# Expert tiles in turns over all experts, with the first batch's pooling begun between the last tiles

## The reference

```python
x = x + mamba4(lap(x))                 # 4 layers: conv, selective scan over the 256 positions, 16 states
r = concat(gelu(x@W1+b1)@W2+b2, h@We[id]+be[id])       # a per-batch conditioned MLP
w, e = top_k(r @ gate, 2); w = softmax(w)              # each token picks 2 of 8 experts
x = x + sum_k w_k * (silu(r@w0[e_k]) * (r@w1[e_k])) @ wo[e_k]
s = tanh(x@cW1+cb1) @ cv                               # pooling logits, one per position
p = softmax(where(mask(kind[b]), s, -1e30)); pooled = p@x / count
x = x + attention(pooled)              # 16 heads of 64, causal, low rank K and V, then @ w_out
c = x@cw[id].T + cb[id]; x = x + bitlinear(gelu(bitlinear(c, w1)), w2)   # ternary weights, 8-bit activations
```

## Time and profile before

| | |
|---|---|
| median of three runs | 1354.98 us (1354.03 to 1356.9) |
| span of the profiled execution, first to last instruction | 1353.1 us |
| busy PE, DVE, ACT, POOL | 1279.3 (95%), 1116.8 (83%), 1019.1 (75%), 1101.0 (81%) us |
| mean granted PE clock | 0.997 |
| scans and routing | 0 to 883 us |
| expert tiles | 883 to 996 us |
| from the last tile to the first projection | 996 to 1017 us |
| attention and last MLP | 1017 to 1353 us |

### The profile page before, as it was taken

One profiled execution on the slowest core, in us unless ns is written; L12 is line 12 of the kernel. 1 busy time (PEld: TensorE's weight loads), 2 busy tenths in 40 slices (PEclk: granted clock), 3 DMA queues, 4 the chain that ended last, 5 costly groups with the idle time before them and its releaser, 6 DMA issues.

```text
span 1353.1 us, 20591 instructions
## 1 busy us (share of the span) xinstructions
PE 1279.3 (95%) x5755; PEld 735.0 (54%) x5764; DVE 1116.8 (83%) x1636; ACT 1019.1 (75%) x2552; POOL 1101.0 (81%) x647
## 2 busy tenths in 40 slices
PE   8899999999999999999999999999998999999997
PEld 4344344344344344344344355789985666676666
DVE  4999999999999999999999989655545566665655
ACT  4888888988988988888888887533326787887785
POOL 5799999999999999999999997454427766857562
PEclk9999999999999999999999999999999999999999
DMA  6564164254254344344435362523221000000000
GB/s 206 224 250 189 64 269 189 88 234 188 103 230 188 138 183 188 153 180 202 173 133 227 164 188 68 156 53 95 69 60 29 9 21 16 22 17 17 9 5 13
DMA packets 48870, 169.49 MB, mean 125 GB/s; under 512 B 15448, under 2 KB 33052, under 8 KB 40460
## 3 DMA queue, kind: packets, MB, share of 16 engines
q1 hardware_dynamic: 46508, 163.81, 31.4%
q0 software_dynamic: 2272, 4.66, 1.6%
HBM read 160.78 MB, written 7.67 MB: 124 GB/s over the span
## 4 chain that ended last, share of the span: by engine, by line
PE 39%; DVE 26%; issue 17%; ACT 12%; POOL 4%; DVEq 1%; DMA 1%; POOLq 0%; ACTq 0%; SPq 0%
DVE h L1479 18%; DVE h L1460 5%; PE banks L424 5%; ACT banks L1441 5%; PE banks L771 4%; PE banks L844 4%; PE banks L818 4%; POOL h L1485 3%; PE banks L433 3%; PE banks L711 2%; PE banks L1514 2%; PE banks L748 2%; PE banks L728 2%; PE banks L859 2%; ACT L1312 2%
## 5 line engine op out<-in xcount | busy, mean ns | idle before, releaser
L1485 POOL TENSOR_TENSOR h<-h,Cb 128x1024 f32<-128x1024 f32 (+2 forms) x166 | 581.5, 3542 | 8.8 <-DVE h L1479 8.3
L1479 DVE TENSOR_TENSOR_SCAN h<-banks,h 128x1024 f32<-128x1024 f32 x256 | 568.7, 2270 | 5.6 <-ACT banks L1441 4.3
L1441 ACT ACTIVATE banks<-dt,A_cur 128x255 f32<-128x255 f32 x1024 | 424.1, 462 | 73.8 <-DVE h L1479 70.9
L1514 PE MATMUL banks<-h,ident 128*128 128x512 f32 x1024 | 471.4, 600 | 4.1 <-DVE yz L1523 1.4
L1514 PEld LDWEIGHTS banks<-h,ident 128*128 128x128 f32 x1024 | 186.7, 190 | 240.0 <-issue 197.6
L1460 DVE TENSOR_TENSOR h<-Bb,banks 128x1024 f32<-128x1024 f32 (+2 forms) x101 | 199.7, 1995 | 0.6
L1466 POOL TENSOR_TENSOR h<-Bb,u 128x1024 f32<-128x1024 f32 (+1 forms) x50 | 184.1, 3685 | 1.9 <-DVE xs L1382 1.8
L810 POOL TENSOR_SCALAR h<-h 128x128 f32<-128x128 f32 (+1 forms) x128 | 97.7, 779 | 53.1 <-DVE h L794 53.1
L810 POOL TENSOR_SCALAR Cb<-Cb,h 128x128 f32<-128x128 f32 x124 | 94.7, 780 | 36.4 <-DVE h L794 36.2
L1268 PE MATMUL banks<-xn,wF 128*128 128x512 f32 x256 | 113.0, 592 | 2.2 <-ACT xn L1260 2.2
L1268 PEld LDWEIGHTS banks<-xn,wF 128*128 128x128 f32 x256 | 47.4, 188 | 63.5 <-issue 60.3
(11 more groups left out here) (393 smaller groups left out, 2048.4 us busy)
## 6 DMA issues: line engine op xcount, KB each, us to landing
Cb<-scrX SPq DMA_DIRECT2D x32, 2048.0 KB, 9.0
Bb<-scrX SPq DMA_DIRECT2D x31, 2048.0 KB, 13.0
h<-in_L_ffn_w SPq DMA_DIRECT2D x2, 2048.0 KB, 8.7
by_expert<-Cb SPq DMA_DIRECT2D x39, 64.0 KB, 1.5
h<-in_conv_w SPq DMA_DIRECT2D x4, 512.0 KB, 4.2
Bb<-scrX SPq DMA_DIRECT2D x2, 1024.0 KB, 5.7
scr<-Cb SPq DMA_DIRECT2D x3, 640.0 KB, 3.0
wF<-scr SPq DMA_DIRECT2D x3, 512.0 KB
```

Of the source, the lines that this page charges most:

```text
L1441: m = e.activation(ps_dA[c % 2][:, g, half, 1:S], dts[q][:, half, i * S + 1:(i + 1) * S], ACT.Exp, scale=A_cur[q][:, s:s + 1])
L1479: e.tensor_tensor_scan(chunk(i, c), ps_dA_flat[c % 2], chunk(i, c), 0.0, ALU.mult, ALU.add).then_inc(sem("scan"), 1)
L1485: e.tensor_tensor(h[i][:, rows(cs), :, :], h[i][:, rows(cs), :, :], both(Cb[i], cs), ALU.mult).then_inc(sem("hC"), len(cs))
L1514: m = e.matmul(bank(5), ident[:], h_flat[i][:, s * HALVES * S:(s + 1) * HALVES * S], start=(s == 0), stop=(s == NS - 1))
```

## The change

Tiles are walked in turns: first the first tile of every expert, then every expert's second, and so on. For that the counting makes, for each pair (expert, n-th list), a number saying whether that list is used and its place in the walk; a comparison with the tile's number and three matmuls give each tile its list and its expert's weights. POOL has three steps instead of six, ACT one copy more, PE one matmul more and five fewer.

A tile's result is stored at the place of its list (read from `tl_col` by SP), not in order of tiles. So a token's place is known from its rank alone, and `dve_homes` is one copy. Tiles without rows go to seven spare places. Before that, 15 DMAs, one in each slot from the second, fill `by_expert` with rows of x (9 places of 64 KB, 590 KB each) on SP's queue behind the second `spread_B`; the first store waits for them.

Since a batch has 256 tokens, its rows are in the first two lists of each expert, so batch 0's lie in the first 16 tiles and batch 1's in the first 32. POOL picks batch 0's rows behind the gathers of tiles 21 and 23, once 16 tiles are stored, and batch 1's behind those of tiles 36 and 38, once 32 are. DVE sums batch 0 behind tile 25 and does its `pmax` before tile 30; PE makes `x2t`, `at` and `S` of batch 0 ahead of `up` of tiles 28, 29 and 30, ACT its parts there. PE waits for what reads banks 4 and 5 before it turns the next tile into them. The hardware loop covers tiles 6 to 17, and tiles 18 to 35 are written out. Two masks and the first conditioned weights are loaded after tile 21.

Behind the last tile PE runs `fold`, `pturn`, `pool`, `q:0`; `heat` and `hold` are gone. `levels`, without its first step, stands on DVE between `pool` and `k:0`. On ACT the exp table and `pexp` stand ahead of `fold`. The slots begin at −2.

```diff
+            def mask(b):
+                kind = e.value_load(ids[0:1, B + b:B + b + 1], min_val=0, max_val=2)
+                wait(e, sem("pch"), 2 * b - 3)
+                dma(chosen[b % 2], layer_of(io["pmask"], kind), f"pk{b % 2}")
+
+            def conditioned(b):
+                sid = e.value_load(ids[0:1, b:b + 1], min_val=0, max_val=NE - 1)
+                wait(e, sem("f_c"), b)
+                dma(fcw, layer_of(io["cw"], sid), "cw")
+                dma(fcb, bass.AP(io["L1_cond2_bias"].tensor, sid * P, [[0, P], [1, P]]), "cw")
+
+            e.wait_ge(sem("table"), 3)
+            e.wait_ge(sem("ys0"), FILLED)
...
             for t in range(TILES):
+                col = e.value_load(tl_col[0:1, t:t + 1], min_val=0, max_val=PLACES - 1)
                 e.wait_ge(sem("mo_o"), t + 1)
-                dma(by_expert[t * P:(t + 1) * P, :], mo_out[t % TRIPLE], f"ys{t % TRIPLE}")
+                dma(layer_of(by_place, col), mo_out[t % TRIPLE], f"ys{t % TRIPLE}")
                 if t == 2 * TRIPLE:
                     dma(f1raw, io["f1t"], "fw_in")
                     dma(f2raw, io["f2t"], "fw_in")
@@ -355,28 +387,19 @@
                 elif t == 6 * TRIPLE:
                     dma(Wq, io["L1_attn_w_q"], "aw_in")
                     dma(Wo, io["L1_attn_w_out"].rearrange("(c p) o -> p c o", p=P), "aw_in")
+                elif t == 7 * TRIPLE:
+                    mask(0)
+                    mask(1)
+                    conditioned(0)
...
+            mask(2)
...
+            e.memset(lists_[:, P:PLACES], 0.0).then_inc(sem("const"), 1)
+            e.wait_ge(sem("const"), CONSTS + 1)
             e.wait_ge(sem("table"), 1)
             for t in range(TILES):
                 k = t % TRIPLE
-                col = e.value_load(tl_col[0:1, t:t + 1], min_val=0, max_val=P - 1)
+                col = e.value_load(tl_col[0:1, t:t + 1], min_val=0, max_val=PLACES - 1)
                 if t == 0:
                     e.wait_ge(sem("by_tok"), 16 * NPAIR)
                     e.wait_ge(sem("table"), 2)
                 wait(e, sem("mo_xt"), t - 2)
                 e.tensor_copy(list_now[:, k:k + 1], lists[:, bass.ds(col, 1)]).then_inc(sem("const"), 1)
-                e.wait_ge(sem("const"), CONSTS + t + 1)
+                e.wait_ge(sem("const"), CONSTS + t + 2)
                 e.indirect_dma_start(xg[k], None, by_token, bass.IndirectOffsetOnAxis(ap=list_now[:, k:k + 1], axis=0)
                                      ).then_inc(sem(f"xg{k}"), 16)
+                if t in GATHER_AFTER:
+                    b, part = divmod(GATHER_AFTER.index(t), 2)
+                    if part == 0:
+                        stored(e, (b + 1) * HALF_TILES)
+                        e.wait_ge(sem("pos"), 1)
+                    gp_gather(e, b, part)
+            stored(e, TILES)
+            run(e, "gp", ATT_GP)
+
+
+        def stored(e, tiles):
             for k in range(TRIPLE):
-                e.wait_ge(sem(f"ys{k}"), 16 * (TILES // TRIPLE))
-            e.wait_ge(sem("pos"), 1)
-            run(e, "gp", ATT_GP)
-
+                e.wait_ge(sem(f"ys{k}"), (0 if k else FILLED) + 16 * len(range(k, tiles, TRIPLE)))
...
+                if isinstance(t, int) and t in FRONT_PE:
+                    PIECES["pe"][FRONT_PE[t]][1](e, 0)
...
+                    if isinstance(t, int) and t in FRONT_READ:
+                        e.wait_ge(sem(FRONT_READ[t][0]), FRONT_READ[t][1])
...
-            with e.Fori(1, TILES // TRIPLE // 2) as j:
+            with e.Fori(1, FRONT // 2) as j:
                 tiles(j * 2, 0)
                 tiles(j * 2 + 1, 1)
+            for j in range(FRONT, TILES // TRIPLE - 1):
+                tiles(j, j % 2)
...
+                    if isinstance(t, int) and t in FRONT_ACT:
+                        PIECES["act"][FRONT_ACT[t]][1](e, 0)
...
+                    if isinstance(t, int) and t == FRONT_MAX:
+                        PIECES["dve"]["pmax"][1](e, 0)
                     tile_mul(t, k, (k + odd) % 2)
                     if not (last and k):
                         tile_weights(t + 2, (k + odd) % 2)
                     if not (isinstance(t, int) and t == 0):
                         tile_out(j - (0 if k else 1), t - 1, (k - 1) % TRIPLE, (k - 1 + odd) % 2)
+                    if isinstance(t, int) and t == FRONT_COMB:
+                        PIECES["dve"]["comb"][1](e, 0)
...
-            weights_levels(e, r)
             e.sem_inc(sem("f_o"), 2)
-            chained.append(r.base + r.k)
-            chained.pop(0)
+            e.wait_ge(sem("fws_ps"), 1)
+            r(e.tensor_scalar(fsm[:, 10:12], bank(5, 2), 1.0 / FF, Q_EPS, ALU.mult, ALU.max))
+            chain[0] = r
+            chained[0] = r.base + r.k + LEVEL_STEPS
             run(e, "dve", ATT_DVE)
 
-        def weights_levels(e, w):
-            e.wait_ge(sem("fws_ps"), 1)
-            w(e.tensor_scalar(fsm[:, 10:12], bank(5, 2), 1.0 / FF, Q_EPS, ALU.mult, ALU.max)); w.sync()
+        def dve_levels(e, b):
+            w = chain[0]
+            w.sync()
...
-            if b == 1:
-                e.wait_ge(sem("x2T"), 2)
-            elif b == 2:
+            if b == 2:
...
+        def front(b, step):
+            return bank(4 if b else 4 + (FRONT_X2T + step) % 2)
...
+            def fill(t):
+                e.dma_start(by_expert[(t - 1) * FILL_PLACES * P:t * FILL_PLACES * P, :], x_rows[0:FILL_PLACES * P, :]
+                            ).then_inc(sem("ys0"), 16)
...
+                    fill(t)
...
             counts = [run_tot[1]] + [tot16[:, t * NE:(t + 1) * NE] for t in range(*GROUPS[2])]
-            row, column = bank(TABLE_BANK)[:, 0:NE], bank(TABLE_BANK)[0:NE, NE:NE + 1]
             for k, here in enumerate(counts):
-                e.matmul(column, here, ones_w[:, 0:1], start=(k == 0), stop=(k == len(counts) - 1))
-            for k, here in enumerate(counts):
-                m = e.matmul(row, ones_w, here, start=(k == 0), stop=(k == len(counts) - 1))
+                m = e.matmul(bank(TABLE_BANK)[0:NE, 2:3], here, ones_w[:, 0:1], start=(k == 0), stop=(k == len(counts) - 1))
...
+        def pe_spread(e, _):
+            e.wait_ge(sem("sums"), 1)
+            e.matmul(bank(TABLE_BANK)[:, 0:1], spread_w, count16, start=True, stop=True).then_inc(sem("rank"), 1)
+
         def pe_ahead(e, _):
-            e.wait_ge(sem("sums"), 1)
-            e.wait_ge(sem("need"), 3)
-            e.matmul(bank(TABLE_BANK)[0:NE, NE + 1:NE + 2], upper_w[0:NE, 0:NE], need16, start=True, stop=True
-                     ).then_inc(sem("rank"), 1)
+            e.wait_ge(sem("sums"), 2)
+            e.wait_ge(sem("need"), 1)
+            e.matmul(bank(TABLE_BANK)[:, 1:2], upper_w, used16, start=True, stop=True).then_inc(sem("rank"), 1)
...
+            n(e.tensor_scalar(used16, counted[:, 0:1], rcon[:, RC_FULL:RC_FULL + 1], None, ALU.is_gt))
+            n(e.tensor_scalar(unused, counted[:, 0:1], rcon[:, RC_FULL:RC_FULL + 1], FAR, ALU.is_le, ALU.mult))
+            e.wait_ge(sem("sums"), 3)
+            n(e.tensor_tensor(turn_no, counted[:, 1:2], unused, ALU.add))
...
+            e.tensor_scalar(hot16, tile_no, turn_no, None, ALU.is_equal).then_inc(sem("need"), 1)
 
         def pe_tiling(e, _):
             e.wait_ge(sem("need"), SPAN_STEPS + 1)
-            e.wait_ge(sem("sums"), 2)
-            got = bank(TABLE_BANK)[:, 2 * NE:2 * NE + 2 * TILES]
-            e.matmul(got[:, 0:TILES], room_w, tq16, start=True, stop=True)
-            e.matmul(got[:, TILES:2 * TILES], ones_w[0:NE, :], tq16, start=True, stop=True).then_inc(sem("rank"), 1)
+            for k, weights in enumerate((ones_w[:, 0:1], place_w, offset_w)):
+                m = e.matmul(tile_table(k), weights, hot16, start=True, stop=True)
...
+        def dve_homes(e):
             e.tensor_copy(pos, place).then_inc(sem("pos"), 1)
...
+            r(e.scalar_tensor_tensor(out=t2[0:1, :], in0=tile_table(0), scalar=-1.0,
+                                     in1=rcon[0:1, RC_SPARE:RC_SPARE + TILES], op0=ALU.add, op1=ALU.mult)); r.sync()
+            e.tensor_tensor(tl_col[0:1, :], tile_table(1), t2[0:1, :], ALU.add).then_inc(sem("table"), 1)
...
+            e.tensor_copy(lists[:, 0:P], bank(LIST_BANK, P)).then_inc(sem("table"), 1)
+            e.tensor_copy(tl_off[0:1, :], tile_table(2)).then_inc(sem("table"), 1)
...
-    pe={-2: "fold heat:36 x2t hold:2 at hold:2 S",
-        -1: """hold:15 pturn pool q:0 k:0 x2t q:1 score:n0 at k:1 S score:n1 q:2 k:2 q:3 score:n2 v:0 k:3 score:n3
+    pe={-2: "fold",
+        -1: """pturn pool q:0 k:0 x2t q:1 score:n0 at k:1 S score:n1 q:2 k:2 q:3 score:n2 v:0 k:3 score:n3
...
-    act={-2: "fold exps x2t at",
-        -1: "pexp pturned q:0 x2t q:1 at k:1 prob:n0 prob:n1 q:2 q:3 prob:n2 prob:n3 v:0 k:3",
+    act={-2: "exps",
+        -1: "pexp fold pturned q:0 x2t q:1 at k:1 prob:n0 prob:n1 q:2 q:3 prob:n2 prob:n3 v:0 k:3",
...
-    dve={-2: "pmax",
```

(19 more changed lines are left out.)

130 lines of the change are left out of this document (57 added, 73 removed).

## The result

The changed kernel took 1348.57 us (median of 6 runs, 1345.57 to 1351.22) beside 1354.26 for the kernel before (6 runs): ratio 0.995, 95% interval 0.9941 to 0.996. It is faster, by 5.7 us, where I forecast 12.4, and it lies above my range. The profiled execution has a span of 1345.9 us and took 1348.85; its span is 7.2 us shorter than that of before.

What follows compares the result with a forecast made beforehand. PE bounds the tile loop and the part from `q:0` on; between them a string of small steps holds `q:0`. Terms −15.1 + 0.6 + 0.7 + 1.4 = −12.4 took 1354.98 to 1342.6 us, range 1339.2 to 1347.

Steps and rivals of the forecast that it cites:

- step 3: Tile loop: PE work of `x2t`, `at` and `S` counts in full, 1.4 us lost, 1.7 at most.
- Step 8: Tile loop: writing out the last loop costs nothing, since PE issued 72 matmuls in 8.20 us of straight code.
- Step 4: Tile loop: DVE, ACT and POOL work is free; tile 37's gather fits by 0.3 us; nothing lost, at most 2.
- a rival for cooling: Behind `fold`: PE cools and its clock falls, loss 1.7 us, time 1344.3; chance 0.10.
- a wait between tiles: Tile loop: tile 37's gather, `pmax` or tanh's table holds PE, loss 1.5 us, time 1344.1; chance 0.10.
- Steps 1 and 2: Behind the last tile: shorter string to `q:0`, 15.1 us gained; `levels` between `pool`'s and `k:0`'s copies, 0.7 lost.
- The lag of ACT's copy: Behind `pturn`: ACT's unexplained 1.24 us wait may stay or go; 0.6 us taken as lost.
- step 2: Behind `q:0`: `levels` delay `score:n0`, 0.7 us lost, bounds 0 and 0.8; a PE gap behind may absorb it.
- more comes: Behind the last tile: no lag of ACT's copy and `levels` absorbed, 1.3 us more, time 1341.3; chance 0.10.
- Steps 5 to 7: SP's queue, tables before tile 0, and 15 fills of 3.7 us in the slots: each costs nothing.
- Tanh: Tile loop: should ACT's tanh need two table switches at tile 29, 2.6 us, no loss; with drain, 1.8 lost.

Runs made afterwards that it cites:

- either edit alone: Kernel before plus four extra POOL gathers behind tiles 21 and 23 (1355.39 us), or with tiles 18 to 35 written out (1355.58 us).
- the kernel with both edits: Kernel before plus four extra POOL gathers behind tiles 21 and 23, and tiles 18 to 35 written out: 1356.70 us, ratio 1.0017.
- the stall with `levels` ahead: `levels` moved ahead of `pool`'s copy on DVE: against the changed kernel 1354.34 us, in the fast order 1351.00 us.
- the fast order: Changed kernel, batch 0's picks singly behind tiles 21 to 24, its sum at 26, batch 1's picks behind 37 and 38, Wq/Wo loads behind 27: 1343.03 us.
- the last three: Changed kernel with 12 tiles written out (1344.56 us), and the fast order with 12 (1340.88 us) and 6 (1340.56 us).

## Why the prediction was wrong

The error is 5.2 us of span, and it is in the tile loop: 7.5 us lost in three places and 0.4 on step 3, less 0.6 at the opening and 2.1 from `fold` to the end, where more was gained than I had put. Without the last two, one of them luck, I would have been further off. The times missed by 0.8 us more (6.0), outside the span: the profiled execution took 2.95 us above its span, where I carried over 1.9.

*Step 8, "the last loop written out. Nothing", failed.* I argued from PE's rate of issue, and never asked where the instructions come from. Even that reading was wrong: 72 matmuls in 8.20 us are 8.8 per us, and a tile asks for 25 (1 + 16 + 8) in 2.79 us, 9.0 per us. In the changed kernel the packets of instructions lie among the gathers and stores of the tile loop. The same change with six tiles fewer written out is faster by 4.0 us in medians, 2.2 us by the two ratios, whose intervals overlap. In the two traces its `q:0` is 3.1 us earlier (1010.75 against 1007.62), though its first three steps were 1.5 us slower. Two ways are told apart. One is shown by its packets: an instruction packet held one DMA engine for 1.4 us, the store's share behind it came that much later, and batch 1's first pick was some 1.6 us late. The other is seen only by where it occurs: ahead of tile 24 one or two of ACT's copies come 1.9 to 3.4 us behind their turns, where 0.3 is usual. They do so in the traces of nine kernels, all with extra gathers or picks in the loop and 18 tiles written out. They don't in the kernel before, with either edit alone, with 12 or 6 tiles written out, or in one build that has both (1343.03). The Trainium skill, "Runtime: NRT & Kernel Launch", section "Instruction fetch mechanics", says that instructions come in blocks of 16 KiB by a DMA queue of the engine's own, mostly hidden, and that kernels prefer full unrolling where possible. The size agrees with one queue of the trace (38 packets of 16 KB); the other has 58 of 8 KB. That it is hidden holds for the written-out loop alone (1355.58 beside 1354.97 for before). It does not hold where POOL waits for a store whose share lies behind such a packet.

*Step 4, "nothing, at most 2", failed as its own margin of 0.3 us warned.* The gather of tile 37 was put at 983.3 and came at 988.61. Tile 31's result was taken at 981.5, not 978.0: the loop came 2.8 us later there, by the first turn, the pieces and tile 24, and I had counted back from the last tile, 0.7 too early even for before. Then store to pick took 4.1 instead of 2.4 (the packet), and the landing some 3.5 us (issue at 988.61, turn at 992.17) instead of 2.49. Two picks went ahead of it and a gather and a pick right behind; that they made it slow is likely, not shown. PE stood idle for 3.35 us, and then came the clock: 2.6 us more at half speed that no rival had. With the picks moved behind tiles 37 and 38, and as much written out, this gap of PE and the half clock were gone. So at tiles 37 and 38, 6.1 of the 7.5 us, it is this step's order of waits that failed; the packet of step 8 gave 1.6 of the wait. I had a rival for cooling, but put it behind `fold`, where the clock was 1.00. The other rival, a wait between tiles, was the right one in kind, at a chance of 0.10 and a price of 1.5 where it cost 6.1 with its clock.

*Step 3* was sized at 1.4 (its own terms, 0.22 + 0.63 + 0.63, make 1.5) and measured 1.8, steps 3.01, 3.53 and 3.61, the same within 0.01 in every variant. `x2t` cost its 0.22; `at` and `S` cost 0.74 and 0.82, with an `up` of 2.05 instead of 1.95 behind each. Why they cost more than in the chain of the kernel before was not tested.

*Steps 1 and 2* held in kind, and both of their losses stayed away. `q:0` starts 6.26 us behind `fold`'s start against 6.6. The lag of ACT's copy, of which I took half, went: the copy starts 0.1 us behind `pturn`. `levels` delay `score:n0` by 1.0 us (4.03 behind `q:0`, 3.01 before), and a gap behind it takes that back, as step 2 allowed: `q:0` to the end is no longer than before. That is the rival "more comes", which happened beside the losses in the loop.

*Steps 5 to 7* held: the run of slots moved as a whole by 0.8 to 1.4 us with the opening, and took 49.76 us a slot with the fills as without them. The start (1.2 us later at the first turn) and the first steps changed from build to build by as much (first turn at 882.3 to 885.2), and I read nothing from them. Tanh cost nothing: the row of L690 stands between two silus, and the trace has no table load between 879.5 and 1002.1 us, so neither switch nor drain.

What stays open: why PE's signals arrive late. The instruction packets that I could place (943.2 to 944.4 and 947.6 to 948.0 us in the kernel with both edits) don't cover the late stretches (938 to 940, 943.8 to 946.5), and the stall with `levels` ahead has no packet in it at all. Open too is why the same picks lost 0, 1.5, 1.4 and 1.4 us around tile 24 in four builds; with 12 or 6 tiles written out the fast order lost 0 in both. As each kernel was traced once, the fault may come and go between executions of one kernel: those of the changed kernel lie up to 5.7 us apart, those of the last three within 2.1.

## What to carry to other kernels

Writing a loop out is not always free where transfers decide: its instructions arrive by DMA in the same stretch. So write out only the tiles that need it, and look for instruction packets beside the transfer that is late. Put a wait of the issuing engine as late in its order as its reader allows. A margin smaller than the spread of a landing is a loss, not a fit; and where PE is the one that waits, look at the granted clock behind the gap, which here cost 2.6 us on top of 3.5. When two edits do nothing alone, test them together too.

## What the runs showed of the hardware

- A 16 KB instruction packet held one DMA engine for 1.4 us, and the nine packets of a 64 KB store on this engine came 0.9 to 1.3 us behind the rest. Over all traces, 16 KB packets between 900 and 1035 us took 0.9 to 1.7 us (median 1.1).
- Behind a gap of PE of 3.35 us the granted clock was 0.50 until 997.8, 6.9 us in all. It fell too with gaps of 2.91 us (the loads behind tile 27) and 3.02 (`levels` ahead). With gaps of 1.92 us (12 tiles written out) and 1.66 (picks behind tile 38) at the same place it stayed at 1.00, but in the kernel with both edits it read 0.50 from 1018.0 on behind one of 1.91, so no limit can be read from these.
- ACT, DVE and POOL can see PE's signals 2 to 4 us late while PE itself keeps its rhythm. It happened in bursts of indirect gathers: with written-out code around them, though not in every such build, and behind eight picks in a row when one DVE step was moved by 3 us (3.7 and 4.1 us late, twice the same).
- With the loop written out and nothing else, a tile's indirect gather of 64 KB landed in 2.5 to 2.6 us in most steps, and in 5.7 and 5.4 us (issued at 943.4 and 946.1) beside two plain loads of 512 KB.
- Tanh ran between two silus with no table load.
